# A two-layer graph attention kernel: two load semaphores, an earlier negation, and reordered first and last slots

## The reference

```python
h = x @ W                                            # layer 0
e = leaky_relu((h @ a_src)[:, None] + (h @ a_dst)[None, :], 0.2)
valid = (adj > 0) & (h.sum(axis=1) != 0)[None, :]
att = where(valid, softmax(where(valid, e, -1e9)), 0)
L, top = valid.sum(axis=1), att.max(axis=1)
att = where(att >= 1e-4, att, 0) * L[:, None]
att = where((top > 1e-4)[:, None], att, 0)
x1 = layernorm(x + elu(h + att @ h))
s = leaky_relu(x1 @ ks.T, 0.2)                       # layer 1
p = softmax(where(adj > 0, s, -9e15))
out = layernorm(x1 + p @ ks)
```

## Time and profile before

| | us |
|---|---|
| median of 3 runs (863.74 to 863.9) | 863.84 |
| the profiled execution's own time | 863.02 |
| its span | 861.2 |
| PE busy | 825.6 (96%) |
| DVE busy | 787.5 (91%) |
| ACT busy | 761.6 (88%) |
| POOL busy | 223.2 (26%) |

### The profile page before, as it was taken

One profiled execution on the slowest core, in us unless ns is written; L12 is line 12 of the kernel. 1 busy time (PEld: TensorE's weight loads), 2 busy tenths in 40 slices (PEclk: granted clock), 3 DMA queues, 4 the chain that ended last, 5 costly groups with the idle time before them and its releaser, 6 DMA issues.

```text
span 861.2 us, 17726 instructions
## 1 busy us (share of the span) xinstructions
PE 825.6 (96%) x7139; PEld 715.4 (83%) x7139; DVE 787.5 (91%) x1004; ACT 761.6 (88%) x731; POOL 223.2 (26%) x446
## 2 busy tenths in 40 slices
PE   6479999999999999999999999999999999999995
PEld 6368887888988888898888888988888898888885
DVE  3988999999999999999999999999999999999744
ACT  3978999999999999999999999999999999999653
POOL 2042133333222233321223233222233321222100
PEclk9699999999999999999999999999999999999998
DMA  9999866667787666678776666886766678620000
GB/s 213 235 130 171 149 97 122 129 132 138 152 153 107 126 125 131 133 148 153 132 115 122 130 131 139 154 152 103 127 127 128 136 149 154 101 41 22 5 1 10
DMA packets 39969, 106.07 MB, mean 123 GB/s; under 512 B 11088, under 2 KB 23504, under 8 KB 32208
## 3 DMA queue, kind: packets, MB, share of 16 engines
q0 software_dynamic: 20864, 66.06, 53.2%
q1 hardware_dynamic: 18592, 38.80, 12.7%
q10 hardware_dynamic: 432, 0.07, 0.0%
HBM read 138.48 MB, written 2.10 MB: 163 GB/s over the span
## 4 chain that ended last, share of the span: by engine, by line
PE 88%; DVE 5%; ACT 3%; issue 3%; DMA 1%; POOL 1%; ACTq 0%; POOLq 0%; DVEq 0%; SPq 0%
PE work L285 24%; PE sums L402 24%; PE sums L426 12%; PE sums L427 6%; PE work L373 6%; PE work L378 6%; PE work L374 6%; DVE att1T L816 1%; DVE att L805 1%; ACT att L587 1%; PE sums L432 1%; DMA a_sb<-a 1%; DMA mask_zero<-zero_cols 1%; PE work L310 1%; DVE att L766 1%
## 5 line engine op out<-in xcount | busy, mean ns | idle before, releaser
L285 PE MATMUL work<-ident,att 128*128 128x128 f32 x2072 | 258.4, 277 | 15.6 <-DVE att L917 11.9
L285 PEld LDWEIGHTS work<-ident,att 128*128 128x128 f32 x2072 | 236.3, 144 | 23.0 <-DVE att L917 12.1
L402 PE MATMUL sums<-h_all,att0T 128*128 128x128 f32 x2048 | 244.3, 275 | 0.0
L402 PEld LDWEIGHTS sums<-h_all,att0T 128*128 128x128 f32 x2048 | 236.2, 192 | 0.0
L426 PE MATMUL sums<-k_parts,att1T 128*128 128x257 f16 x1024 | 182.4, 274 | 1.2 <-DVE res L827 0.8
L427 PE MATMUL sums<-k_parts,att1T 128*128 128x129 f16 x1024 | 177.3, 218 | 0.0
L597 ACT ACTIVATE att1T<-work 128x1024 f16<-128x1024 f32 x128 | 130.9, 1027 | 36.3 <-PE work L285 36.3
L816 DVE SCALAR_TENSOR_TENSOR att1T<-work,att1T 128x1024 f16<-128x1024 f32 x128 | 152.4, 1211 | 5.1 <-ACT att1T L597 5.0
L805 DVE CUSTOM_DVE_ANT_0 att<-att,mask 128x2048 f32<-128x2048 f32 x64 | 146.4, 2290 | 2.4 <-ACT att L582 2.4
L766 DVE SCALAR_TENSOR_TENSOR att<-att,cut 128x2048 f32<-128x2048 f32 x62 | 145.4, 2349 | 0.0
L582 ACT ACTIVATE att<-work 128x1024 f32<-128x1024 f32 x128 | 127.4, 1026 | 19.4 <-PE work L378 19.4
(11 more groups left out here) (118 smaller groups left out, 653.2 us busy)
## 6 DMA issues: line engine op xcount, KB each, us to landing
mask<-adj POOLq DMA_DIRECT2D x31, 1024.0 KB, 8.6
mask_zero<-zero_cols SPq DMA_DIRECT2D x29, 1024.0 KB, 5.1
mask_zero<-adj POOLq DMA_DIRECT2D x29, 1024.0 KB, 11.6
att<-x SPq DMA_DIRECT2D x4, 512.0 KB, 6.7
k_parts<-ks POOLq DMA_DIRECT2D x2, 1024.0 KB, 18.0
x_sb<-x SPq DMA_DIRECT2D x32, 64.0 KB, 2.7
out<-x SPq DMA_DIRECT2D x32, 64.0 KB, 4.9
mask<-adj POOLq DMA_DIRECT2D x2, 512.0 KB, 6.7
```

Of the source, the lines that this page charges most:

```text
L285: mm = pe.transpose(place[:, b * P:(b + 1) * P], source(c * PER + b), ident[:, :])
L402: mm = pe.matmul(acc0, att0T[:, k * P:(k + 1) * P], h_all[:, k, :], start=(k == 0), stop=(k == BLOCKS - 1))
```

## The change

`small_in` becomes `w_in` and `a_in`, and the vector's matmul goes behind the second chunk of x. In `FIRST` each fill names its place; h 5 comes before z 2. `negate_k` moves from slot 0 to among the quarters of the first cut, GpSimd's `add_adj(3)` behind the k load and `deviation0(0)` ahead of `offset0(2)`. The lists up to slot 2 are reordered on TensorE, ACT and DVE, `zero_mask(4)` goes into slot 1, `zero_mask(5)` behind `offset1` in slot 3. Slots 30 and 31 get lists of their own: all four `sum1` of tile 30 come after the last score, and the last tile's mask and exponential go by quarters, with the high parts of chunks 2 and 3 made on DVE instead of ACT. `BY_VECTOR = (2, 3)` names those chunks. Where a line below has twelve columns of indentation, they are taken off.

```diff
-        small_in, kall_in = sem("small_in"), sem("kall_in")
+        w_in, a_in, kall_in = sem("w_in"), sem("a_in"), sem("kall_in")
...
-        FIRST = (("x", 0), ("x", 1), ("h", 0), ("x", 2), ("h", 1), ("x", 3), ("h", 2), ("z", 0), ("d", 0), ("h", 3),
-     ("z", 1), ("d", 1), ("h", 4), ("z", 2), ("d", 2), ("h", 5), ("z", 3), ("d", 3))
-        FIRST_PLACES = SLOTS + 1
+        FIRST = (("x", 0, 0), ("x", 1, 1), ("h", 0, 2), ("x", 2, 3), ("h", 1, 0), ("x", 3, 1), ("h", 2, 2), ("z", 0, 3),
+     ("d", 0, 0), ("h", 3, 1), ("z", 1, 2), ("d", 1, 3), ("h", 4, 0), ("h", 5, 3), ("z", 2, 1), ("d", 2, 2),
+     ("z", 3, 0), ("d", 3, 1))
...
-pe.wait_ge(small_in, 48)
+pe.wait_ge(w_in, 16)
 pe.transpose(wT_ps, w_sb[:, 0:D], ident[:, :]).then_inc(wT_made, 1)
 first_fill(0)
+first_fill(1)
+pe.wait_ge(a_in, 32)
 pe.wait_ge(a_one_ready, 1)
 pe.wait_ge(wT_ready, 1)
 pe.matmul(v_ps, wT_sb[:, :], a_sb[:, :], start=True, stop=True).then_inc(v_made, 1)
-for n in range(1, len(FIRST)):
+for n in range(2, len(FIRST)):
...
-    pe.wait_ge(exp1, 2 * u + 1 + c // 2)
+    pe.wait_ge(exp1, 2 * u + 1 + (c // 2 if u < TILES - 1 else c))
...
 def first_slot():
-    for c in range(CHUNKS):
-        turn0(0, c)
+    turn0(0, 0)
+    turn0(0, 1)
     sum0(0, 0)
+    turn0(0, 2)
+    turn0(0, 3)
+    sum0(0, 1)
     turn_k(0)
-    for c in range(1, CHUNKS):
-        sum0(0, c)
-    for c in range(1, CHUNKS):
-        turn_k(c)
+    sum0(0, 2)
+    sum0(0, 3)
+    turn_k(1)
+    turn_k(2)
+    turn_k(3)
     turn_q(0)
...
     sum0(1, 0)
+    sum0(1, 1)
     turn0(1, 3)
-    sum0(1, 1)
     sum0(1, 2)
     turn1(0, 0, True)
     turn1(0, 1, True)
     sum0(1, 3)
     turn1(0, 2, True)
+    turn1(0, 3, True)
     sum1(0, 0)
-    turn1(0, 3, True)
     sum1(0, 1)
...
     turn0(2, 3)
+    sum1(0, 3)
     sum0(2, 1)
-    sum1(0, 3)
     turn1(1, 0, True)
...
 def last_slots():
-    u, w = TILES - 1, TILES - 2
-    score(u, 3)
-    sum1(w, 2)
-    sum1(w, 3)
+    t = TILES - 2
+    score(t - 1, 3)
     for c in range(CHUNKS):
-        turn1(u, c, False)
+        turn0(t, c)
+    for c in range(3):
+        sum0(t, c)
+    turn1(t - 1, 0, True)
+    sum0(t, 3)
+    sum1(t - 2, 2)
+    sum1(t - 2, 3)
+    for c in range(1, CHUNKS):
+        turn1(t - 1, c, True)
+    turn_q(t)
+    sum1(t - 1, 0)
     for c in range(CHUNKS):
-        sum1(u, c)
+        score(t, c)
+    t = TILES - 1
+    sum1(t - 2, 1)
+    turn0(t, 0)
+    sum1(t - 2, 2)
+    turn0(t, 1)
+    turn0(t, 2)
+    sum0(t, 0)
+    sum0(t, 1)
+    turn1(t - 1, 0, True)
+    turn0(t, 3)
+    sum0(t, 2)
+    sum0(t, 3)
+    sum1(t - 2, 3)
+    turn1(t - 1, 1, True)
+    turn1(t - 1, 2, True)
+    turn_q(t)
+    turn1(t - 1, 3, True)
+    for c in range(CHUNKS):
+        score(t, c)
+    for c in range(CHUNKS):
+        sum1(t - 1, c)
+    for c in range(CHUNKS):
+        turn1(t, c, False)
+    for c in range(CHUNKS):
+        sum1(t, c)
...
-nc.scalar.dma_start(w_sb[:, 0:D], W).then_inc(small_in, 16)
+nc.scalar.dma_start(w_sb[:, 0:D], W).then_inc(w_in, 16)
 for i in range(2):
-    nc.scalar.dma_start(a_sb[:, i:i + 1], a[i * D:(i + 1) * D, :]).then_inc(small_in, 16)
+    nc.scalar.dma_start(a_sb[:, i:i + 1], a[i * D:(i + 1) * D, :]).then_inc(a_in, 16)
...
+def last_raise1(k):
+    act.wait_ge(bias1_ready, TILES)
+    nc.scalar.activation(att1[:, quarter(k)], att1[:, quarter(k)], ACT.Exp,
+                         bias=bias1[(TILES - 1) % 2][:, :]).then_inc(exp1, 1)
...
 def to_first_slot():
     keep_x(0)
     keep_x(2)
+    keep_zero(0)
     keep_parts(2)
     keep_h(2)
-    keep_zero(0)
     keep_d(0)
     keep_parts(3)
-    keep_h(3)
     keep_zero(1)
     keep_d(1)
+    keep_h(3)
     keep_parts(4)
     keep_h(4)
+    keep_parts(5)
     keep_zero(2)
-    keep_parts(5)
     keep_d(2)
     keep_zero(3)
     keep_d(3)
@@ -641,48 +691,59 @@
     first_raise0()
 def first_slot():
+    keep_h(5)
+    copy0(0, 0)
     bend0(1)
-    keep_h(5)
+    copy0(0, 1)
+    copy0(0, 2)
+    copy0(0, 3)
     raise0(1, 0)
-    copy0(0, 0)
-    copy0(0, 1)
+    k_high_part(0)
     raise0(1, 1)
-    copy0(0, 2)
-    k_high_part(0)
-    copy0(0, 3)
-    bend0(2)
     elu_exp(0)
     k_high_part(1)
     k_high_part(2)
+    k_high_part(3)
     q_high_part(0)
-    k_high_part(3)
-    raise0(2, 0)
+    bend0(2)
     for c in range(CHUNKS):
         bend1(0, c)
-def early_slot(t):
...
+def early_slots():
+    copy0(1, 0)
+    copy0(1, 1)
+    copy0(1, 2)
+    raise0(2, 0)
+    raise1(0, 0)
+    copy0(1, 3)
+    raise1(0, 1)
+    copy1(0, 0)
+    copy1(0, 1)
+    copy1(0, 2)
+    elu_exp(1)
+    copy1(0, 3)
+    raise0(2, 1)
+    q_high_part(1)
+    bend0(3)
     for c in range(CHUNKS):
-        bend1(t, c)
+        bend1(1, c)
+    copy0(2, 0)
+    copy0(2, 1)
+    raise0(3, 0)
+    copy0(2, 2)
+    raise1(1, 0)
+    raise1(1, 1)
+    copy0(2, 3)
+    copy1(1, 0)
+    raise0(3, 1)
+    elu_exp(2)
+    copy1(1, 1)
+    copy1(1, 2)
+    copy1(1, 3)
+    q_high_part(2)
+    bend0(4)
+    for c in range(CHUNKS):
+        bend1(2, c)
...
-def last_slot():
-    u = TILES - 1
-    raise1(u, 0)
-    raise1(u, 1)
+def last_slots():
+    t = TILES - 2
+    copy0(t, 0)
+    raise0(t + 1, 1)
+    copy0(t, 1)
+    copy0(t, 2)
+    raise1(t - 1, 0)
+    copy0(t, 3)
+    raise1(t - 1, 1)
+    elu_exp(t)
+    copy1(t - 1, 0)
+    copy1(t - 1, 1)
+    q_high_part(t)
+    copy1(t - 1, 2)
+    copy1(t - 1, 3)
     for c in range(CHUNKS):
-        copy1(u, c)
+        bend1(t, c)
+    t = TILES - 1
+    copy0(t, 0)
+    copy0(t, 1)
+    copy0(t, 2)
+    raise1(t - 1, 0)
+    raise1(t - 1, 1)
+    copy0(t, 3)
+    copy1(t - 1, 0)
+    elu_exp(t)
+    copy1(t - 1, 1)
+    q_high_part(t)
+    copy1(t - 1, 2)
+    copy1(t - 1, 3)
+    for c in range(CHUNKS):
+        bend1(t, c)
+    last_raise1(0)
+    last_raise1(1)
+    last_raise1(2)
+    copy1(t, 0)
+    copy1(t, 1)
+    last_raise1(3)
...
+def last_mask1(k):
+    u = TILES - 1
+    dve.wait_ge(bent1, 4 * u + k + 1)
+    nc.vector.tensor_tensor_reduce(att1[:, quarter(k)], att1[:, quarter(k)], mask[u % MASKS][:, quarter(k)],
+                                   1.0, -3.0e38, ALU.add, ALU.max,
+                                   first_top[:, k:k + 1]).then_inc(masked1, 1)
+def last_offset1():
+    u = TILES - 1
+    dve.wait_ge(masked1, 2 * u + QUARTERS)
+    nc.vector.tensor_reduce(bias1[u % 2][:, :], first_top[:, :], AX.X, ALU.max,
+                            negate=True).then_inc(bias1_ready, 1)
+def last_high1(c):
+    u = TILES - 1
+    dve.wait_ge(turned1, 4 * u + c + 1)
+    dve.wait_ge(summed1, 4 * (u - 1) + c + 1)
+    nc.vector.tensor_scalar(high1T[:, cols(c)], work[:, (2, 0, 1, 2)[c], :], LIFT, None,
+                            ALU.mult).then_inc(last_copied1, 1)
+def offset1(u):
+    dve.wait_ge(masked1, 2 * u + 2)
+    nc.vector.tensor_reduce(bias1[u % 2][:, :], top1[u % 2][:, :], AX.X, ALU.max,
+                            negate=True).then_inc(bias1_ready, 1)
 def low_part1(u, c):
-    dve.wait_ge(copied1, 4 * u + c + 1)
+    if u < TILES - 1 or c not in BY_VECTOR:
+        dve.wait_ge(copied1, 4 * u + c + 1)
+    else:
+        dve.wait_ge(last_copied1, BY_VECTOR.index(c) + 1)
...
 def to_first_slot():
     keep_x(1)
+    keep_h(0)
     keep_parts(0)
-    keep_h(0)
     keep_parts(1)
+    keep_h(1)
     test_zero(0)
-    keep_h(1)
     keep_x(3)
+    first_build(0)
     test_zero(1)
-    first_build(0)
     first_build(1)
     first_mask0(0)
     test_zero(2)
-    build_mask(1)
     first_mask0(1)
     test_zero(3)
+    build_mask(1)
     first_mask0(2)
     first_mask0(3)
+    zero_mask(1)
     dve.wait_ge(first_topped, QUARTERS)
     nc.vector.tensor_reduce(top0[0][:, :], first_top[:, :], AX.X, ALU.max).then_inc(masked0, 1)
     first_offset0(0)
-    zero_mask(1)
     mask0(1)
     first_threshold0()
+    first_cut(0)
+    first_cut(1)
+    first_cut(2)
+    negate_k()
+    build_mask(2)
+    first_coefficient()
+    first_cut(3)
+def first_slot():
+    zero_mask(2)
     first_offset0(1)
-    for k in range(QUARTERS):
-        first_cut(k)
-
-def first_slot():
-    build_mask(2)
-    zero_mask(2)
     mask0(2)
-    first_coefficient()
     k_low_part(0)
-    threshold0(1)
-    negate_k()
     residual0(0)
     elu(0)
     k_low_part(1)
     normalise0(0)
     q_low_part(0)
     k_low_part(2)
+    threshold0(1)
     k_low_part(3)
     cut(1, 0)
     cut(1, 1)
-def early_slot(t):
...
+def early_slots():
+    mask1(0, 0)
+    mask1(0, 1)
+    offset1(0)
+    zero_mask(3)
+    mask0(3)
+    low_part1(0, 0)
+    residual0(1)
+    low_part1(0, 1)
+    elu(1)
+    low_part1(0, 2)
+    normalise0(1)
+    zero_mask(4)
+    threshold0(2)
+    q_low_part(1)
+    low_part1(0, 3)
+    cut(2, 0)
+    cut(2, 1)
+    mask1(1, 0)
+    mask1(1, 1)
+    offset1(1)
+    mask0(4)
+    finish1(0)
+    build_mask(3)
+    low_part1(1, 0)
+    residual0(2)
+    threshold0(3)
+    elu(2)
+    low_part1(1, 1)
+    normalise0(2)
+    low_part1(1, 2)
+    q_low_part(2)
+    low_part1(1, 3)
+    cut(3, 0)
```

(64 more changed lines are left out.)

79 lines of the change are left out of this document (20 added, 59 removed).

## The result

The changed kernel took 855.85 us (median of 4 runs, 854.86 to 858.11) against 863.79 (862.63 to 863.9) for the kernel before, measured beside it: a ratio of 0.9915, 95% interval 0.9893 to 0.9936. The forecast was 858.1 with a range from 855.6 to 862.2. The execution that was profiled is the slowest of the four, 858.11 with a span of 856.3. Against the 861.2 of before that is 4.9 less; the sum had said 5.7.

What follows compares the result with a forecast made beforehand. TensorE, without idle time from 167.4 to 814 us, bounds the kernel; only head and tail can move. Head 3.5, slots 1 to 3 0.8 and tail 1.4 sum to 5.7: 863.02 becomes 857.3, as median 858.1; range 855.6 to 862.2.

Steps and rivals of the forecast that it cites:

- the forecast's own range: Range of the main forecast case alone, 856.8 to 860.3 us, given a chance of 0.55.
- Head 1: TensorE's start: with two semaphores the first h begins 1.2 us earlier, of which 0.9 is left behind DVE.
- if it stays put, 0.5 is lost: Case at TensorE's start: the clock's rise does not move with the earlier start, losing 0.5 us.
- Head 2: Reordered work around the first cuts: cuts start at 36.4 instead of 37.78, y of tile 0 0.9 us earlier.
- Head 3: GpSimd's deviation of tile 0 no longer behind the k load's issue: 2.5 us more won, x1 at 56.15.
- Slots 1 to 3: TensorE's waits in these slots with the reordered lists: 1.9 us lost against 2.7, so 0.8 won.
- Tail: Last two slots and drain: 1.4 us won, last sum at 854.0 instead of 855.4.
- Clock kept: Rival: TensorE's clock holds through the shorter wait for x1, 1.5 us more won, 856.6; chance 0.13.
- The third mask lands late: Rival: add_adj(3) behind the k load delays zero_mask(3) in slot 1; 866.6; chance 0.07 with other such mishaps.
- if `zero_mask(3)` waits for a DMA: Sign of being wrong: DVE's third mask in slot 1 waits for its load to land.
- The other signs: TensorE wait over 1 us in slots 1 to 3, DVE over 1.5 behind ending slot 3, drain low-part wait over 1.

Runs made afterwards that it cites:

- again: The changed kernel once more, nothing edited: 855.94 us, ratio 0.9898.
- one_sem: The changed kernel with TensorE waiting for W and both vector halves before its first transpose, vector's matmul behind the first x chunk again: 857.17 us, ratio 0.9915.
- late_k: The changed kernel with negate_k, add_adj(3) and the deviation of tile 0 back in their old places: 860.00 us, ratio 0.9952.
- the pair with the bend moved: The kernel before with bend0(2) behind k's last cast and q's on ACT, with the k part (862.94 us) and without it (865.26 us).
- bend_only: The kernel before with only bend0(2) moved behind k's last cast and q's on ACT: 865.26 us, ratio 1.0020.
- fill_q: The changed kernel with 12 dummy transposes on TensorE between the last transpose of the keys and that of q: 857.33 us, ratio 0.9922.
- fill_both: The changed kernel with 12 dummy transposes ahead of q, 16 ahead of W, and add_adj(3) issued ahead of the k load: 853.97 us, ratio 0.9889.
- old_tail: The changed kernel with the old lists for slots 30, 31 and the drain: 856.98 us, ratio 0.9915.
- add_first: The changed kernel with add_adj(3) issued ahead of the k load instead of behind it: 855.91 us, ratio 0.9910.
- fill_start: The changed kernel with 16 dummy transposes on TensorE while it waits for W: 855.29 us, ratio 0.9899.

## Why the prediction was right, and where its terms were off

The forecast (858.1) was right in sign and in size: the sum of 5.7 met 4.9 in the same kind of trace, and 7.9 in the medians. In the profiled execution the parts that were off made up for each other: the head and slots 1 to 3 gave 0.1 more than forecast (4.39 for 4.3), the tail 0.8 less. The median (855.85) lies below the forecast's own range (856.8 to 860.3) and only 0.25 above the lower end of the whole one. It got there by a start at which full rate comes earlier, which the prediction did not have; that this still fell inside the range is luck.

**Head 1, the start: mis-sized both ways.** I let 1.2 through, less 0.3 behind DVE. In the profiled execution the clock's rise did not move with the start: the third x chunk was turned at 12.64, ACT had its last `d` 0.4 earlier (26.89 for 27.32), and the cuts began 0.92 earlier instead of 1.4. That is the case "if it stays put, 0.5 is lost". In `again` the rise came some 4 us earlier and the cuts began at 34.79, 3.0 earlier than in before. The term is therefore either 0.9 or 3.0 at the cuts, by when TensorE reaches full rate. `one_sem` and `again`, both with an early rise, tell the two apart: of the 3.0 the two semaphores and the moved matmul of the vector are worth 1.6 (34.79 for 36.37), and 1.2 at the end; the other 1.4 is the early rise and the new order together. The usual one is the larger, and its 2.1 us make nearly all of the 2.25 by which the median lies below my forecast.

**Head 2** held: from the first cut to y it took 16.18 (16.45 by my walk), so y came 0.72 earlier (0.9) although the cuts were 0.46 late; the bend of tile 2 began at 57.13 (57.1) and ended at 60.84 (60.9).

**Head 3** held: mv to deviation 0.27 (within 0.3), y to x1 3.16 (3.3), x1 at 56.20 (56.15). `late_k` has the term at 2.68 and the pair with the bend moved at 2.3, for 2.5. What I had only half seen is that it is not a term by itself: alone on the kernel before it is worth 0.4, which is not clear of nothing. In the walk I wrote "ACT is free for the exponential" and took it as given, while that was the work of another edit (the bend behind q), which by itself costs 2.0 (`bend_only`) and pays only with the rewritten slot 1. That last step is argued: slot 1's list was never run alone.

**Slots 1 to 3** held as a sum: the change gained 1.23 between slot 1 and slot 4, where I had 0.8 (+0.05 in slot 1, -0.38 in slot 2, +1.56 in slot 3, which lasts 25.64 for 27.20). In slot 3 the waits of 0.50 and 0.83 are gone and the one for x1 is 0.32. No run took `zero_mask(5)` or these lists back by themselves, so this term rests on the two traces.

**Tail: less than half as large.** The slots 30 and 31 took 49.51 us for 49.75, and the last score ended at 834.21 (834.1); the hole is 1.32 (1.25), and no half rate is left behind it. The failing step is the drain: DVE's six parts began 7.5 after the last score and ended at 14.65 instead of at 14.2, and the last sum ended 1.58 behind them instead of 1.4. The slots themselves gained 0.2 where I had 0.4.

```profile
841.73 2.36 DVE L937 SCALAR_TENSOR_TENSOR att1T<-work,att1T 128x1024 f16<-128x1024 f32 x2 [0.45 <-ACT att1T L647]
844.00 1.22 DVE L924 TENSOR_SCALAR att1T<-work 128x1024 f16<-128x1024 f32 x1
847.64 1.22 DVE L937 SCALAR_TENSOR_TENSOR att1T<-work,att1T 128x1024 f16<-128x1024 f32 x1
```

So the last sum came 16.2 after the last score (15.6 forecast, 16.6 before), and the tail gained 0.6 instead of 1.4.

**The rivals.** *Clock kept* is false as worded: the clock still fell in the scores, in both traces. That keeping it wins 1.3 at that place (1.5 forecast) is shown by three kernels: from x1's turn to slot 1 it took 6.60 in `fill_q` and 6.61 in `one_sem` and `fill_both`, but 7.92 in both traces of the change and in `old_tail`, `add_first` and `fill_start`. *The third mask lands late* is true as a mechanism and harmless in size: it took 25.5, so 69.65, where I had put the strictly serial bound at 69.4 and its wanted time at 69.4 too (it was wanted at 69.07). It cost DVE 0.62 and TensorE nothing here, but slot 1 was 0.6 to 1.0 longer where it began early for the mask's issue (`one_sem`, `fill_q`). I leaned on the 16.4 of an add issued 7.5 us behind the load; issued 2.2 behind it, it took 25.5 and landed 7.4 after the load. The Trainium skill, "DMA: Bandwidth & Descriptors", section "Issuing engines are not separate DMA queues", has such transfers interleave; that fits the load's own 20.3 for 16.6, but it gives no size. My sign that it would be wrong "if `zero_mask(3)` waits for a DMA" was therefore too strict. The other signs stayed away: TensorE's longest wait in slots 1 to 3 is 0.32, DVE ends slot 3 ahead of TensorE (137.11 and 137.99), and no wait for a low part in the drain reaches 0.3.

## What to carry to other kernels

A wait on a chain through three engines is worth what the second latest of its inputs allows: before such a term is summed, walk the list of each engine that feeds the chain, and ask which other edit has emptied it. Freeing one queue (GpSimd) gained 0.4 us alone, hardly clear of nothing, and 4.1 together with ACT's new lists. And where a kernel ends on one engine without a gap, what is lost or won in its first microseconds is carried whole to its end, so the clock of the start is worth a try with cheap filler work: 28 idle transposes and one reordered load together took 1.5 to 1.9 us off. By the traces 1.3 of it is the full rate in the scores and 0.7 the start, while the reordered load alone gave nothing. The spread was 0.3 over four executions of `fill_both`, against 3.3 over eight of the change (1.2 without the late one); four are few.
